# Mixing between two banks of queries, variances in two parts, and a load of the keys that waits for four banks

## What is computed

```python
x = x + L0_conv(ln_c(x), qkv_w, qkv_b, proj_w, proj_b, rel_height, rel_width)
t = to_tokens(x); t = t + L0_ffn(ln_t(t), W1, b1, W2, b2); x = from_tokens(t, x)
x = x + L1_conv(ln_c(x), f_w, f_b, v_w, v_b, proj_w, proj_b, sim_alpha, sim_beta)
t = to_tokens(x); t = t + L1_ffn(ln_t(t), W1, b1, W2, b2); x = from_tokens(t, x)

# L0_conv, per window and head
attn = softmax(q @ k.T + rel_pos_emb(q)); out = proj(attn @ v)
# L1_conv, per fold and head
sim = sigmoid(beta + alpha * l2norm(centres) @ l2norm(points).T)
sim = sim * (own centre is argmax)
agg = (sim @ value + value_centers) / (sum(sim) + 1)
out = proj(agg.T @ sim)
# FFN
h = relu(q_acc(q_mul(z) @ q_mul(W1) + q_mul(b1))); y = q_acc(q_mul(h) @ q_mul(W2) + q_mul(b2))
```

## Time and profile before

| | us |
|---|---|
| median of 3 runs | 9042.88 |
| lowest, highest | 9035.99, 9101.01 |
| the profiled execution | 9053.59 |
| its span in the trace | 9051.6 |
| TensorE busy (matmuls) | 7854.1 (87%) |
| TensorE busy (weight loads) | 6323.5 (70%) |
| VectorE busy | 6910.7 (76%) |
| ScalarE busy | 4896.1 (54%) |
| GpSimd busy | 2503.7 (28%) |
| mean granted TensorE clock | 0.899 of full speed |

### The profile page before, as it was taken

The page is one execution under the profiler, slowest core; times in us unless marked ns, Lnnn a source line. Parts: engine busy times, 40 slices in busy tenths (PEclk is TensorE's granted clock), DMA queues, the critical chain, the costliest instruction groups (busy, mean ns, idle before and its releaser), DMA issues.

```text
span 9051.6 us, 429211 instructions
## 1 busy us (share of the span) xinstructions
PE 7854.1 (87%) x172050; PEld 6323.5 (70%) x172050; DVE 6910.7 (76%) x22530; ACT 4896.1 (54%) x9750; POOL 2503.7 (28%) x4860
## 2 busy tenths in 40 slices
PE   6999999998899899988989889998898989897555
PEld 4777777777777777777777777777777777775433
DVE  3676777877888887777887778777888778887666
ACT  2444444545555565555655555555565555655445
POOL 1333333333333323223232223322323223332000
PEclk7998999989999999999999999999999999998555
DMA  2111111111222222222222222222222222221111
GB/s 57 40 42 42 44 51 46 51 51 54 58 61 57 57 60 56 61 58 55 61 64 55 56 58 58 55 59 58 57 58 62 57 54 61 58 61 53 56 54 60
DMA packets 193342, 501.73 MB, mean 55 GB/s; under 512 B 33508, under 2 KB 67108, under 8 KB 191468
## 3 DMA queue, kind: packets, MB, share of 16 engines
q1 hardware_dynamic: 191692, 476.75, 19.3%
HBM read 228.84 MB, written 169.93 MB: 44 GB/s over the span
## 4 chain that ended last, share of the span: by engine, by line
PE 69%; DVE 15%; issue 9%; ACT 6%; DMA 1%; SPq 0%; ACTq 0%; DVEq 0%; POOL 0%; POOLq 0%
PE scores_x L703 10%; PE bank L662 6%; PE flipped L725 6%; PE pv L753 4%; PE bank L665 4%; DVE maxes L1570 3%; PE bank L673 3%; PE misc L616 3%; PE bank L962 3%; PE pv L747 3%; PE scores_x L643 3%; PE bank L607 3%; PE misc L782 3%; DVE shifted L1578 2%; PE bank L680 2%
## 5 line engine op out<-in xcount | busy, mean ns | idle before, releaser
L2046 POOL TENSOR_TENSOR vrest<-vstage,vmask 96x384 f32<-96x384 f32 x512 | 437.6, 855 | 4615.4 <-ACT vstage L1199 4615.4
L1570 DVE TENSOR_REDUCE maxes<-scores_x 128x6 f32<-128x864 f32 x1024 | 1076.8, 1052 | 780.1 <-PE scores_x L703 775.6
L703 PE MATMUL scores_x<-keys,queries 64*64 64x144 f32 x24576 | 1070.7, 307 | 133.3 <-DVE shifted L1578 66.5
L665 PE MATMUL bank<-xn,wq 97*32 97x64 f32 x24576 | 961.8, 233 | 138.9 <-issue 137.8
L662 PE MATMUL bank<-xt,wq 97*32 97x64 f32 x24576 | 941.9, 233 | 127.1 <-issue 115.0
L703 PEld LDWEIGHTS scores_x<-keys,queries 64*64 64x64 f32 x24576 | 786.8, 142 | 378.5 <-issue 343.3
L662 PEld LDWEIGHTS bank<-xt,wq 97*32 97x32 f32 x24576 | 814.9, 118 | 262.3 <-issue 237.8
L1578 DVE TENSOR_TENSOR shifted<-scores_x,maxes 128x768 f32<-128x768 f32 x1024 | 969.4, 947 | 0.5
L665 PEld LDWEIGHTS bank<-xn,wq 97*32 97x32 f32 x24576 | 828.5, 117 | 151.9 <-issue 151.8
L1187 ACT ACTIVATE queries<-bank 128x512 f32<-128x512 f32 x768 | 458.8, 597 | 864.6 <-PE bank L665 862.4
L725 PE MATMUL flipped<-ident,shifted 128*128 128x128 f32 x6144 | 895.3, 284 | 0.2 <-ACT vstage L1199 0.2
(11 more groups left out here) (193 smaller groups left out, 17382.9 us busy)
## 6 DMA issues: line engine op xcount, KB each, us to landing
keys<-kst SPq DMA_DIRECT2D x768, 99.0 KB, 3.6
x_in<-x_dram SPq DMA_DIRECT2D x130, 396.0 KB
xn_kept<-xn SPq DMA_DIRECT2D x128, 388.0 KB, 2.5
later<-xn_kept SPq DMA_DIRECT2D x128, 388.0 KB, 3.4
x_tok<-tok_dram SPq DMA_DIRECT2D x128, 384.0 KB, 3.1
x_kept<-x SPq DMA_DIRECT2D x128, 384.0 KB, 2.4
later<-x_kept SPq DMA_DIRECT2D x128, 384.0 KB, 3.6
out_dram<-later SPq DMA_DIRECT2D x128, 384.0 KB, 2.4
```

What stands on the lines that cost most here:

```text
L665: last = mm(dst[64 * e + 32:64 * e + 64, :, j, :], wq[0:PROW, 2 * WS + j, 2 * g + e, :], rows[:, j], start=True, stop=True, skip_group_che ...
L703: last = mm(score[e][64 * j:64 * j + 64, g * NKEY:(g + 1) * NKEY], queries[64 * e:64 * e + 64, g, w, :], keys[64 * e:64 * e + 64, g, :, WS ...
L1570: V.tensor_reduce(maxes[:, p % 2, :, :], sc, AX.X, ALU.max).then_inc(max_ready.sem, 1)
```

## The change

- **Mixing.** `mix(n, 0)` and `mix(n, 1)` of TensorE leave iteration 5 and stand in the queries: the first between banks 2 and 3, the second behind bank 4. They write to `fill` instead of `work` and wait there for `hc_evac`. VectorE's `mix` moves from iteration 6 to the strip's end, ahead of `best_of`. The first two banks of queries wait no longer for `mixed`; `make_values(n, 1, fill)` does.
- **Variances.** Parts 0 and 1 move from iteration 3, ahead of the flip, to the end of iteration 2; part 2 stays.
- **Mean.** `mean(n+1, 1)` moves behind the flips of iteration 0.
- **First FFN.** `flip_z(n-1, 1)` moves from behind flip and weigh of iteration 2 to its head, with `store_z` of ScalarE and `ffn_apply` of VectorE (into iteration 1).
- **ScalarE, iteration 4.** `quantise` 4 and 5 go ahead of `store_sims`.
- **Keys.** `load_keys(n+1)` waits also for `q_ready.at(n+1, 4)`: four of the six banks of queries.

```diff
                 sp.sem_inc(gate, 1)
+                sp.wait_ge(q_ready.sem, q_ready.at(n, 4))
+                sp.sem_inc(gate, 1)
                 sp.wait_ge(s_ready.sem, s_ready.at(n, 0))
...
                     pe.wait_ge(q_stored.sem, q_stored.at(n, i - 1))
-                elif on and on.c1:
-                    pe.wait_ge(mixed.sem, mixed.at(n - 1, i + 1))
                 if g == 0:
...
                             pe.wait_ge(hc_evac.sem, hc_evac.at(n - 1, 6))
+                        if on.c2:
+                            pe.wait_ge(mixed.sem, mixed.at(n - 1, 2))
                         make_values(n, 1, fill)
...
                         mean(n + 1, 0)
-                        mean(n + 1, 1)
                     if p == 1 and ahead:
                         mean(n + 1, 2)
+                    if p == 2 and b1:
+                        if on.b:
+                            pe.wait_ge(ft_ready.sem, ft_ready.at(n, 2))
+                        flip_z(n - 1, 1)
                     if p == 2 and on.b:
...
                     if p == 3 and ahead:
-                        for c in range(3):
-                            variance(n + 1, c, on)
+                        variance(n + 1, 2, on)
                     if p == 4:
...
                         flip_heads(0)
-                        if on.c1:
-                            pe.wait_ge(mixed.sem, mixed.at(n, 2))
                         if ahead:
...
                     if p == 0:
+                        if ahead:
+                            mean(n + 1, 1)
                         if on.c3:
...
                         flip_features(n, 0, k % 2)
-                    if p == 2 and b1:
-                        if on.b:
-                            pe.wait_ge(ft_ready.sem, ft_ready.at(n, 2))
-                        flip_z(n - 1, 1)
+                    if p == 2 and ahead:
+                        variance(n + 1, 0, on)
+                        variance(n + 1, 1, on)
                     if p == 3 and on.c2:
...
                             pool(n - 2)
-                        if on.c1:
-                            pe.wait_ge(v_stored.sem, v_stored.at(n, 8))
-                            mix(n, 0)
-                            mix(n, 1)
                     if b1 and p in (1, 2, 3):
...
                 if ahead:
-                    make_queries(n + 1, 0, on)
+                    make_queries(n + 1, 0)
                     make_keys(n + 1, 2)
-                    make_queries(n + 1, 1, on)
+                    make_queries(n + 1, 1)
+                if on.c1:
+                    if on.c2:
+                        pe.wait_ge(hc_evac.sem, hc_evac.at(n, 5))
+                    mix(n, 0, fill)
+                if ahead:
+                    make_queries(n + 1, 2)
                 flip_heads(1)
                 if ahead:
-                    make_queries(n + 1, 2)
                     make_queries(n + 1, 3)
+                if on.c1:
+                    if on.c2:
+                        pe.wait_ge(hc_evac.sem, hc_evac.at(n, 6))
+                    mix(n, 1, fill)
                 project(1)
...
 
-            def mix(n, u):
+            def mix(n, u, dst):
                 pe.wait_ge(st_ready.sem, st_ready.at(n, 1))
-                mm(work[u][:, 0:4 * C], simw_t[:, u, :], mix_w[:, :, :].rearrange("p t c -> p (t c)"),
+                mm(dst[u][:, 0:4 * C], simw_t[:, u, :], mix_w[:, :, :].rearrange("p t c -> p (t c)"),
                    start=True, stop=True).then_inc(mix_ready.sem, 1)
...
                 if not on.ahead:
-                    if on.c2:
-                        pe.wait_ge(hc_evac.sem, hc_evac.at(n, 6))
+                    pe.wait_ge(hc_evac.sem, hc_evac.at(n, 6))
+                    pe.wait_ge(mixed.sem, mixed.at(n, 2))
                     flip_z(n, 0)
...
                         pe.wait_ge(zct_ready.sem, zct_ready.at(n, 2))
-                    mix(n, 0)
-                    mix(n, 1)
+                    mix(n, 0, work)
+                    mix(n, 1, work)
                 if on.b:
...
                     if p == 2:
+                        if b1:
+                            store_z(n - 1, 1)
                         if ahead:
...
                     if p == 2 and b1:
-                        store_z(n - 1, 1)
                         hidden(n - 1, 2)
...
                     if p == 4:
+                        if b1:
+                            quantise(n - 1, 4)
+                            quantise(n - 1, 5)
                         if on.c1:
...
                         if b1:
-                            quantise(n - 1, 4)
-                            quantise(n - 1, 5)
                             output(n - 1, 0)
...
                         ffn_normalise(n - 1, 1, False, on.c2)
-                    if p == 2 and b1:
                         ffn_apply(n - 1, 1)
...
                     if p == 6:
-                        if on.c1:
-                            mix(n, 0, par)
-                            mix(n, 1, par)
                         if b1:
...
                     hidden_c(n, 5)
+                if on.c1:
+                    mix(n, 0, par, fill)
+                    mix(n, 1, par, fill)
                 if on.b:
...
 
-            def mix(n, u, par):
+            def mix(n, u, par, src):
                 dve.wait_ge(mix_ready.sem, mix_ready.at(n, u + 1))
...
                 V.tensor_tensor(xc[par][:, 4 * u:4 * u + 4, :], xc[par][:, 4 * u:4 * u + 4, :],
-                                work[u][:, 0:4 * C].rearrange("p (t c) -> p t c", c=C), ALU.add
+                                src[u][:, 0:4 * C].rearrange("p (t c) -> p t c", c=C), ALU.add
                                 ).then_inc(mixed.sem, 1)
...
                 if on.c1:
-                    mix(n, 0, par)
-                    mix(n, 1, par)
+                    mix(n, 0, par, work)
+                    mix(n, 1, par, work)
                 if on.b:
```

## The result

| | before | after |
|---|---|---|
| median, us | 9039.43 | 9524.51 |
| lowest, highest | 9024.75, 9101.01 | 9495.5, 9536.32 |
| span of the profiled execution | 9051.6 | 9493.5 |
| mean granted clock | 0.899 | 0.87 |

The changed kernel takes 1.0522 times as long as the kernel before, 95% interval [1.0482, 1.0563]. The prediction was 8925 us; the result lies outside its range (8780 to 9090) and is slower than its slower rival (9175).

What follows compares the result with a forecast made beforehand. TensorE bounds the kernel (69% of the chain), with VectorE close in stretches 0 to 3. -1.5 us in 94 full strips and +0.65 in 34 early ones give -119 us: 8925 us, range 8780 to 9090.

Steps and rivals of the forecast that it cites:

- slower rival: Keys' wait eats the gain, half of the strips beginning at half clock: +133 us, 9175; chance of over 1% slower 0.15.
- Item 8: Strip's start: the keys' wait idles TensorE, so one in ten more strips begins at half clock; +0.2 us (0 to 2.2).
- Item 7: Strip's end: scores(0) waits longer for the keys, whose load now waits for four query banks; +1.75 us (1.2 to 2.3).
- item 3: Variances split over stretches 3 and 4: the clock no longer falls as much; 0.7 us gained (nothing to 1.0).
- Item 2: `flip_z` ahead of features and flip(2): TensorE's hole before the second `hidden` matmul closes; 0.6 us gained (0 to 0.9).
- item 1: Mean moved behind flip(0), into a 0.78 us hole; `ffn_apply` now precedes pair 2's reduction: worth 0 (at most 0.28 us).
- Item 4: ScalarE's `quantise` 4 and 5 before `store_sims`, shortening TensorE's hole before `output`; 0.75 us gained (0.5 to 0.9).
- list of signs: What would show it: keys' wait 1 to 2.5 us a strip, L937's wait under 0.4, stretch 5 near 5.3 us.
- item 5: Mix leaves stretch 5, so scores(7) starts earlier; 1.4 us gained (1.0 to 2.0).
- item 6: Queries: two mixes of 0.7 us each, hidden in instruction waits and behind the keys' wait; cost 0 (up to 1.4).
- second rival: Gain and wait cancel: first mix costs 0.7 us in the queries, or the clock gives nothing; 9015 us, chance 0.28.
- VectorE's `best_of`: Strip's end: mix ahead of `best_of` makes simw late despite 1.8 us of slack; at most 1 us a strip, 9020.

Runs made afterwards that it cites:

- e10: e6 with the load of the keys also waiting for four of the six banks of queries: 9599.6 us, 1.0602 of the kernel before.
- e6: Kernel before with only the mixing moved and ScalarE's `quantise` 4 and 5 ahead of `store_sims`: 8798.3 us, 0.9718 of the kernel before.
- e16: Changed kernel, but the keys wait for two banks of queries and GpSimd waits with its sums for `ffn_apply`: 8618.5 us, 0.9529 of the kernel before.
- e17: e12 with GpSimd waiting with its sums for `ffn_apply`: 8755.7 us, 0.968 of the kernel before.
- e2: Changed kernel without the new wait of the keys' load: 1.0100 of the kernel before.
- e9: e6 with VectorE's `ffn_apply` moved ahead of pair 2's reduction, as in the change: 9046.6 us, 0.9997 of the kernel before.
- e15: e9 with GpSimd waiting before its sums until `ffn_apply` is done, order unchanged: 8837.6 us, 0.9799 of the kernel before.
- e7: Kernel before with only the mixing moved as in the change: 8875.6 us, 0.9826 of the kernel before.
- e12: e6 with the keys' load waiting for two banks of queries: 8771.3 us, 0.968 of the kernel before.
- e13: e9 with GpSimd's two sums moved behind its third masking of values: 1.02 of the kernel before.
- e11: e10 with twelve matmuls of no use ahead of the gather, filling TensorE's wait: 9053.3 us, 0.9996 of the kernel before.
- e4: Changed kernel with twelve matmuls of no use ahead of the gather, while TensorE waits for the keys: 9330.0 us, 1.0286 of the kernel before.
- e1: Kernel before with only the keys' load also waiting for four of six banks of queries: 9746.4 us, 1.0774 of the kernel before.

## Why the prediction was wrong, step by step

Figures are of full strips; those of the prediction stand first.

- **Item 8, the clock behind the wait: +0.2 (0 to 2.2); measured +4.8** (head of e10 against e6). This is the step that turned the sign. It failed twice. The count: I took one strip in ten, but all 85 full strips of the changed kernel and of e10 begin at half clock, 13 of 85 before and 5 of 85 in e6. The length: the upper end priced stretch 0 alone, 5.3 us, while the half clock ran on into stretch 1, 12.6 us in the mean. The price of 0.41 us for each was right: 4.8 us for 11.8 more. The earlier trace rows held a stretch 0 at 0.50, and the prediction takes it as a rare event; for "one in ten more" behind a longer wait it names no row.
- **Item 7, the wait itself: +1.75 (1.2 to 2.3); measured +2.1** (stretch 7 of e10 against e6), +2.0 in the changed kernel. Right, by landing and issue times from the earlier trace rows.
- **Items 1 to 3, the mean, the first FFN and the variances: 0 - 0.6 - 0.7 = -1.3.** With GpSimd's hold-up out of the way, e16 against e17, they gave -1.8 (62.6 to 60.9): -2.1 in stretch 4, where the clock is restored as item 3 said (half clock 2.9 to 0.8 us; 8 of 12 variances are also gone from the stretch), -0.7 in the head, +1.0 in stretches 2 and 3. Item 2's hole did close: no wait of `hidden` for z8t is left in the changed kernel (80.2 us, 127 times before). With the hold-up they lost: e2 is 2.9 us a full strip over e6. The step that failed is item 1's "worth 0": `ffn_apply` was priced at its 1.16 us from the earlier trace rows, against 1.2 us of slack before scores(3). Both numbers are right for that strip, but the price was of the old place. In the new place VectorE works beside GpSimd's sums and masking and needs 1.3 us more (`ffn_apply` 2.6 us in e2 and e9, 1.3 in e15), so the slack of full strips is overdrawn. No row of GpSimd stands behind the prediction.
- **The early strips** were given the same items. They have no such slack: in the kernel before scores(3) starts there 0.15 us after shifted(2) in the mean, that is, at once (1.3 us in full strips). They grew by 7.8 us each in the changed kernel instead of 0.65: 3.7 in the head and 2.4 in stretch 7, which are items 7 and 8 again, and 4.5 in stretches 2 and 3, less 2.8 in stretches 4 to 6. The price of each item was read from full strips only.
- **Item 4, quantise ahead of store_sims: -0.75; measured -0.84** (e6 against e7). Right on that base. In the changed kernel itself `output` still waits for `quantise` 0.7 us a case (fence below; 0.3 in e6), where the prediction's list of signs wanted under 0.4, and stretch 5 is 6.5 us, against 6.2 in e6 and 7.0 before.
- **Items 5 and 6, the mixing: -1.4 and 0; together measured -1.75** (e7 against before). Of this 1.4 are in stretch 6, as item 5 priced them; stretch 7, where the two mixes now stand, grew by 0.1 us only, as item 6 took it, and not by the 1.4 that would follow if their price had to be paid there (the second rival, which named this, took 0.7). TensorE's "issue" waits before the query matmuls fell from 253 to 182 us in e7. The rest of the gain, 0.5 us, is in the head, whose half clock fell from 1.9 to 0.7 us; no item forecast that, and no run here explains it, so that much of the nearness is luck. The prediction's list of signs put this gain in stretch 5; by its own definition the mixing stood in stretch 6, which fell from 6.4 to 5.0 us. The wrong name changed no sum.
- **VectorE's `best_of`** as a rival: it is late. The slack of 1.8 us was not there: ahead of the gather TensorE waits for simw 70 times, 20 before, and in the full strips 0.7 us in the mean. It costs the changed kernel no time that shows, since the keys come later still; in e7, with 65 such waits and no wait for the keys, stretch 7 as a whole is only 0.1 us longer.
- **The slower rival** named the right mechanism, but took half of the strips, and for each of them stretch 0 only, 1.1 us a strip; all 85 begin slow, with 10.3 us at half clock in the changed kernel and 12.6 in e10.

The waits for `quantise`, before, in the changed kernel and in e6, and for simw, before and in the changed kernel:

```profile
PE flipped L937 <- ACT h L1317: 106.1, 121, 1.1
...
PE flipped L945 <- ACT h L1327: 86.2, 117, 1.3
...
PE flipped L940 <- ACT h L1321: 22.6, 71, 0.9
...
PE pv L972 <- DVE simw L1821: 121.1, 20, 7.0
...
PE pv L980 <- DVE simw L1830: 157.4, 70, 7.0
```

The sum of the prediction without items 7 and 8 is -3.45 in 94 strips and -1.3 in 34, -368 us, 8675 us on the median's scale; e16, which is the change without their causes and without the hold-up, took 8618. That the two are so near is in part luck: full strips fell by 4.7 us instead of 3.45, and early ones grew by 1.7 instead of falling by 1.3.

In the changed kernel the two causes overlap. From e16 to it a full strip grows by 6.6 us: 3.9 in the head, 2.4 in stretch 7 and only 0.3 between, since there the slow head gives VectorE time. An early strip grows by 6.1 (2.4, 2.6 and 1.1), those between (19 to 32) by 10.0 (4.8, 2.1 and 3.1).

What stays open: why the wait for two banks leaves the early strips' heads slower in e12 and e17 (10.6 and 10.4 us against 9.7) though not in full ones, and why early strips of e16 still have 3.4 us of half clock in stretch 3. No run separates these.

## What to carry to other kernels

A wait of TensorE can cost its length and then the half clock behind it: here 2.1 us of waiting cost 6.9. So price every new wait with the slow stretches that follow, in all the strips in which it occurs, and fill it with real work (or start the transfer earlier) rather than shorten it. Before an instruction of VectorE is moved to another time, read GpSimd's timeline at that time: its duration in the old place is no price for the new one. Read the slack in each kind of strip, not in one; and test the parts of a change one by one, since two losses that overlap hid here a version that is 4.7% faster.

## What the runs showed of the hardware that was not expected

- VectorE's Newton instructions of 0.17 us took up to 1.46 us beside GpSimd's two-operand instructions and copies (e13), and the 0.32 us instructions of `ffn_apply` up to 1.0 (e9) and 1.6 (e13). Beside GpSimd's `TENSOR_SCALAR xn<-x,mr` the Newton instructions were hardly held up: over the whole of e9 they took 0.18 us at the median and 0.44 at most, against 0.17 with GpSimd idle. The port that one engine holds for a whole instruction, as cited above, does not show there.
- Holes in TensorE's work came before slow stretches much longer than themselves: 2.5 us in the mean in front of scores(0) in e10 (and 0.7 ahead of the gather), with 12.6 us at half clock behind; 1.8 us in front of scores(3) in e2, with 5.5 us in stretch 3. With a filler in the first hole (e11) 8 of 85 strips begin slow; the 1.2 us of hole in the mean that the filler left did no harm in full strips.
- Half clock in one place can spare another: in full strips, with the head slow, stretch 3 of the changed kernel had 0.0 us of it, with the head filled (e4) 4.5 us.
- The query matmuls stood on "issue" for 253 us in the kernel before. With the keys' load held back for four banks and nothing else changed it was 191 us (e1), and from e6 to e10, by the same edit, it fell from 174 to 94. So the load has a part in these holes, as the prediction took it; what they are made of no run shows, and moving the mixing alone (e7) brought them down to 182.
